# Loading and splitting attention's output weight inside attention instead of in the weights' part

## The reference

```
x = x + L0_xattn(layernorm(x), ctx, ctx)    # 16 heads of 32, softmax, with Wq, Wk, Wv, Wo, biases, temperature
x = x + L0_ffn(layernorm(x))                # 512 -> 2048 -> 512, weights and activations rounded to 8-bit steps
x = x + L1_xattn(layernorm(x), ctx, ctx)    # no softmax: scores * values, residual and layernorm inside
x = x + L1_ffn(layernorm(x))                # three 512 x 512 products, then tanh
```

## Time and profile before

| | us |
|---|---|
| median of three runs | 1871.63 |
| the profiled execution, its own time | 1874.35 |
| its span in the trace | 1872.6 |
| PE busy | 1791.1 (96%) |
| DVE busy | 1549.5 (83%) |
| ACT busy | 1239.9 (66%) |
| POOL busy | 954.1 (51%) |
| `prepare` / `attend` / `rest`, from first to last instruction | 0 to 172.0 / 172.3 to 945.9 / 947.4 to 1872.6 |

### The profile page before, as it was taken

One profiled execution on the slowest core, in us unless ns is written; L12 is line 12 of the kernel. 1 busy time (PEld: TensorE's weight loads), 2 busy tenths in 40 slices (PEclk: granted clock), 3 DMA queues, 4 the chain that ended last, 5 costly groups with the idle time before them and its releaser, 6 DMA issues. The chain is left out here.

```text
span 1872.6 us, 30344 instructions
## 1 busy us (share of the span) xinstructions
PE 1791.1 (96%) x9447; PEld 1345.5 (72%) x9530; DVE 1549.5 (83%) x3607; ACT 1239.9 (66%) x3379; POOL 954.1 (51%) x1053
## 2 busy tenths in 40 slices
PE   8997899999999999999879999899999999999997
PEld 7785688888888888888744444467677677767775
DVE  6765789999999999998769888888888888888875
ACT  4564899999999999999633333356555555565543
POOL 3121466666666666666610000156676666766664
PEclk9998999999999999999989999999999999999999
DMA  8377234544444444433379999064445445444311
GB/s 292 135 235 219 64 100 116 133 124 113 116 130 125 116 117 129 126 93 94 88 240 386 403 401 382 26 249 147 160 166 173 168 145 190 166 142 171 124 47 40
DMA packets 146927, 308.47 MB, mean 165 GB/s; under 512 B 44496, under 2 KB 56784, under 8 KB 129104
## 3 DMA queue, kind: packets, MB, share of 16 engines
q1 hardware_dynamic: 146624, 306.26, 50.3%
q10 hardware_dynamic: 144, 0.26, 0.1%
HBM read 165.95 MB, written 106.95 MB: 146 GB/s over the span
## 5 line engine op out<-in xcount | busy, mean ns | idle before, releaser
L1246 POOL TENSOR_TENSOR a_pr<-a_pr,a_rcp 128x512 f32<-128x512 f32 x256 | 266.8, 1042 | 283.2 <-DVE a_rcp L1092 283.0
L1002 ACT ACTIVATE a_pr<-a_s,a_nmax 128x128 f32<-128x128 f32 x1024 | 364.8, 381 | 15.7 <-DVE a_nmax L1085 14.0
L1495 PE MATMUL f_pair<-f_room,w 128*128 128x512 bf16 x999 | 224.6, 382 | 2.6 <-ACT f_room L1606 1.3
L1002 ACT ACTIVATION_READ_ACCUMULATOR a_pr<-a_s,a_nmax 128x1 f32 x1024 | 225.1, 220 | 0.0
L1937 POOL TENSOR_TENSOR f_ring<-f_ring,f_room 128x512 f32<-128x512 f32 x64 | 82.0, 1281 | 245.0 <-DVE f_room L1882 245.0
L1718 DVE CUSTOM_DVE_ANT_0 f_hf<-f_pair,nb,sh 128x512 f32<-128x512 f32 x244 | 172.0, 749 | 29.5 <-PE f_pair L1495 23.2
L1100 DVE TENSOR_TENSOR a_pTl<-a_pt,a_pTh 128x512 fp32r<-128x512 f32 x256 | 168.7, 680 | 19.8 <-ACT a_pTh L1014 19.1
L1085 DVE TENSOR_REDUCE a_nmax<-a_s 128x4 f32<-128x512 f32 x256 | 172.8, 675 | 13.9 <-PE a_s L892 13.6
L1495 PEld LDWEIGHTS f_pair<-f_room,w 128*128 128x128 bf16 x1024 | 99.4, 98 | 116.4 <-issue 3.0
L1650 ACT ACTIVATE f_room<-f_ring,f_off,f_rs 128x512 f32<-128x512 f32 x128 | 104.1, 813 | 114.2 <-POOL f_off L1928 113.3
L1922 POOL TENSOR_TENSOR f_rs<-f_rs,f_half 128x1 f32<-128x1 f32 x128 | 72.2, 564 | 187.2 <-DVE f_rs L1771 187.2
(11 more groups left out here) (392 smaller groups left out, 5141.6 us busy)
## 6 DMA issues: line engine op xcount, KB each, us to landing
hidden<-f_hf SPq DMA_DIRECT2D x57, 1024.0 KB, 9.4
f_hf<-hidden SPq DMA_DIRECT2D x57, 1024.0 KB, 5.2
xb<-x SPq DMA_DIRECT2D x16, 1024.0 KB, 5.7
a_qs<-bqreph SPq DMA_DIRECT2D x128, 128.0 KB, 2.4
a_qs<-bqrepl SPq DMA_DIRECT2D x128, 128.0 KB, 2.4
a_xr<-x SPq DMA_DIRECT2D x64, 256.0 KB, 3.7
x<-a_xr SPq DMA_DIRECT2D x64, 256.0 KB, 2.5
f_ring<-x SPq DMA_DIRECT2D x64, 256.0 KB, 4.8
```

What stands on the lines that cost most here:

```text
L1002: last = e.activation(pr[:, t, j, :], s_bank[t][:, j * P:j * P + P], ACT.Exp, bias=nmax[kk % 2][:, t, j:j + 1], accum_out=sums[kk % 2][:, ...
L1246: e.tensor_tensor(p, p, rcp[kk % 2][:, t, :].unsqueeze(2).to_broadcast([P, 4, KEYS]), ALU.mult).then_inc(*e_pn)
L1495: last = e.matmul(h_bank[(PAIRS * u + i) % 3][:, q, :], w1[:, k, f * P:f * P + P], xT[u % 2][:, k, :], start=k == 0, stop=k == KC - 1)
```

## The change

`WoT0` leaves the weights' part: the load, ACT's copy of 128x2048 and DVE's subtraction of 128x2048 go. Attention's SP issues it as four quarters of 256 KB into `xr[0..3]`, behind the first query tile's four transfers. ACT waits at the opening of step 0 for the four quarters and for `bo` together (one semaphore now counts all five transfers), and copies four tiles of 128x512 into `woh`. DVE makes the four low halves in step 3. Nothing else reads the `xr` tiles before: SP's first reload of x and PE's first output product wait for the low halves. In `rest` the four semaphores of the first tokens' quarters become one, which counts all four, so every quarter's relu waits for all of them.

In the weights' part, the lists of loads and slots:

```
-                 plain("A2"), w2_rows(3), x_rows[0], plain("WT"), plain("WqT0"), x_rows[1], plain("WoT0"), x_rows[2]]
-        BUF = [i % 3 for i in range(20)] + [0, 1, 2]
-        X_LOAD = {20: scr["e_x"][1], 22: scr["e_x"][0]}
+                 plain("A2"), w2_rows(3), x_rows[0], plain("WT"), plain("WqT0"), x_rows[1], x_rows[2]]
+        BUF = [i % 3 for i in range(20)] + [0, 2]
+        X_LOAD = {20: scr["e_x"][1], 21: scr["e_x"][0]}
```

and there ACT's call, DVE's call, and SP's loads ahead of and behind the eight stores:

```
-            weight(9, place["t"][-1])
...
-            weight(9)
...
-            load(21)
...
-            load(22)
+            load(21)
```

In attention, the semaphores, PE's `out`, ACT's `step`, DVE's `step` (behind `norm`), SP's `again` and SP's opening:

```
-        e_const, e_b = ev("const"), ev("bias", 16)
+        e_const, e_b, e_woh, e_wol = ev("const"), ev("outweight", 16 * (KC + 1)), ev("outhi"), ev("outlo")
...
+                if first(b) and o == 0:
+                    e_wol.wait_ge(e, KC - 1)
...
                 if opening:
+                    e_b.wait_ge(e, 0)
+                    for c in range(KC):
+                        e.activation(wo[0][:, c, :], xr[c][:], ACT.Copy).then_inc(*e_woh)
                     qhi(b, kk)
...
+                if first(b) and kk == 3:
+                    for c in range(KC):
+                        e_woh.wait_ge(e, c)
+                        e.tensor_tensor(wo[1][:, c, :], xr[c][:], f32(wo[0][:, c, :]), ALU.subtract).then_inc(*e_wol)
                 rc(b, kk, 1)
                 smax(b, kk, 2)
...
+                if first(b) and o == 0:
+                    e_wol.wait_ge(e, KC - 1)
...
             paired(0, -QUERY)
+            for c in range(KC):
+                e.dma_start(xr[c][:], A["WoT0"][cut(c), :]).then_inc(e_b.sem, 16)
             body_steps(e, step, LOAD, STORE + 1)
```

In `rest`, the semaphore, ACT's wait ahead of a relu, and SP's load of a quarter:

```
-        e_tok0, e_relu0 = [ev(f"first{t}", 16) for t in range(TPG)], ev("relu0")
+        e_tok0, e_relu0 = ev("first", 16 * TPG), ev("relu0")
...
-                        e_tok0[t].wait_ge(e, 0)
+                        e_tok0.wait_ge(e, 0)
...
-                e.dma_start(xb[0][:, t, :], x_g[0][:, t, :]).then_inc(*e_tok0[t])
+                e.dma_start(xb[0][:, t, :], x_g[0][:, t, :]).then_inc(e_tok0.sem, 16)
```

More of the change, by code:

```diff
@@ L116, in prepare @@
                  w1_rows(0), w1_rows(1), w1_rows(2), w1_rows(3), w2_rows(0), w2_rows(1), w2_rows(2), plain("A1T"),
-                 plain("A2"), w2_rows(3), x_rows[0], plain("WT"), plain("WqT0"), x_rows[1], plain("WoT0"), x_rows[2]]
-        BUF = [i % 3 for i in range(20)] + [0, 1, 2]
-        X_LOAD = {20: scr["e_x"][1], 22: scr["e_x"][0]}
-        W_LOAD, W_SLOT = (2, 3, 4, 5, 6, 14, 15, 18, 19, 21), (1, 2, 0, 1, 2, 0, 1, 2, 1, 0)
+                 plain("A2"), w2_rows(3), x_rows[0], plain("WT"), plain("WqT0"), x_rows[1], x_rows[2]]
+        BUF = [i % 3 for i in range(20)] + [0, 2]
+        X_LOAD = {20: scr["e_x"][1], 21: scr["e_x"][0]}
+        W_LOAD, W_SLOT = (2, 3, 4, 5, 6, 14, 15, 18, 19), (1, 2, 0, 1, 2, 0, 1, 2, 1)
         W_CENTRED = W_LOAD.index(5)
@@ L987, in _ @@
         def _(e):
-            e.dma_start(bo[:], A["L0_xattn_bo"].rearrange("(a n) -> a n", a=1).to_broadcast([P, D])).then_inc(*e_b)
+            e.dma_start(bo[:], A["L0_xattn_bo"].rearrange("(a n) -> a n", a=1).to_broadcast([P, D])).then_inc(e_b.sem, 16)
             def xhi(b, kk):
```

## The result

The changed kernel took 1880.27 us (median of 18 runs, 1875.31 to 1884.29), the kernel before 1874.32 us in the same series (18 runs, 1870.16 to 1879.64): 5.95 us more, a ratio of 1.0031 with a 95% interval of 1.0023 to 1.0039. The ratio lies just over the bound of 0.3% which the prediction had set for "slower". A second series gave 1881.71 against 1874.71, ratio 1.0036 (1.0024 to 1.0048). The sign was forecast; the size was three times the forecast +1.9.

The account below looks back on a forecast made before the run. Early attention steps are paced by a chain through ACT, DVE and PE, later ones by a full PE. Opening -1.0, step 3 +0.8 and `rest` +2.1 sum to +1.9: 1871.63 + 1.9 = 1873.5 us, range 1869.5 to 1877.8.

Parts of the forecast that it names:

- PE's clock: At attention's opening, PE stands still and restarts at the lower clock level as before; put at 0.
- Weights' part: End of the weights' part: without WoT0's copy and subtraction the border comes at 168.25, 4.0 us earlier.
- Opening: Attention's step 0: ACT waits for the weight's quarters, then copies; `qhi` begins 1.0 us earlier, bounds -3.7 to +1.9.
- Rival B: Attention's opening: fourth quarter lands at 182.95 behind a full queue; sum +7.4, 1879.0 us; chance 0.06.
- Rival A: Attention's opening: quarters land early, at 174.7, giving -3.7 there; sum -0.8, 1870.8 us; chance 0.14.
- Step 3: Attention's step 3: four added DVE subtractions, 2.48 us in a row, cost +0.8 us, bounds 0 to 1.75.
- the next 0.57 us have no more slack to go into: Attention's step 3: DVE work beyond the 1.91 us that `norm` takes in step 2 comes out in full.
- 0.24 + 0.57: Attention's step 3: 0.24 us that `norm` cost in step 2 plus the next 0.57 us, making +0.8.
- The weighing of POOL against DVE: Attention's step 3: POOL's overlap loses DVE 0.1 us; under an exclusive lock up to 1.04, the term +1.8.
- Opening of `rest`: Start of `rest`: four relus begin only when the fourth token quarter lands, +2.1 us, bounds 0.8 to 2.1.
- Rival C: Step 3 and `rest`'s opening: waits behind take up the added 0.8 or 2.1; sum -1.0, 1870.6 us; chance 0.10.
- A stage away from these three places: Rest of the kernel: no change forecast; one of over 2 us there would show the prediction wrong.

## Why the prediction was off, step by step

The sign was right and three of the terms held (border, plain delay of step 3, tokens). Two steps failed. The opening's term was mis-sized: -1.0 forecast, +0.2 measured in the table and +0.8 over more profiles. And PE's clock was put at nothing outside the opening, without a reason: behind step 3 a lowered clock added 0, 1.3 or 3.1 us in the three profiles, and at the end of attention, a place with no term at all, it stands beside +1.9 us.

**Weights' part: -4.0, right.** (-4.2 measured.) From the last fold to attention's first transfer the changed kernel takes 12.1 us, the kernel before 16.3.

**Opening: -1.0 forecast, +0.2 measured in the table; mis-sized.** (Counted with the kernels that share the opening, four profiles on either side, it is +0.8.) The mechanism (ACT waits for the weight, then copies) was right and the landing was wrong. Counted from attention's first transfer, the text had the fourth quarter issued at 3.8 us, landing at 9.1 and `qhi` at 11.1. Measured: 4.25, 10.64 and 12.73. Of the 1.6 us, 0.45 is the issue (the fourth quarter went 1.7 us behind the first, not the 1.3 of the earlier trace rows), 1.1 the landing (6.4 us against 5.25 of the earlier trace rows) and the rest the copies. The tokens' quarters were the nearest row by size, but they meet an idle queue; WoT0's stand behind x's third group, with the DMA share at 1.04 in 174 to 178. Rival B named that queue and overrated it. Rival A, an early landing, was not seen in any profile. The late copies recovered 4.7 us: with the border's -4.2 that leaves about +0.5 for the opening as the change has it, beside the +0.2 and +0.8 above.

**Step 3: +0.8 forecast; the plain part right, the clock left out.** `xlo` of step 3 came 12.30 us after that of step 2 (text: 12.2), and a step without lowered clock is 0.92 us longer. So the premise that "the next 0.57 us have no more slack to go into" held. The step that failed is the sum behind it, 0.24 + 0.57, which made the price a plain delay: I had asked about PE's clock at the opening alone, and with the lowered clock the two steps were 2.4 us longer in the mean of three profiles instead of 0.9. By the runs the block alone costs 2.2 us, and spreading it out saves 2.3. PE also shows a wait that was not there before: its transposes wait 0.66 us for POOL's product, which waits for the reciprocal behind the four. It comes shortly before the 1.66 us that PE stands for `xlo` anyway:

```profile
226.21 0.66 PE L902 MATMUL a_pt<-ident,a_pr 128*128 128x128 f32 x4 [0.66 <-POOL a_pr L1252]
228.96 0.50 PE L61 MATMUL a_qx<-a_xT1h,wqh 128*128 128x512 f32 x1 [1.66 <-DVE v1l L1081]
```

That this wait tips the clock is not shown: the wait is the same in the profile whose clock stayed at 1.00. The weighing of POOL against DVE there changed nothing: POOL's product ran from 221.55 to 222.59, the four began at 222.39 and took 2.55 us against the 2.48 of the earlier trace rows.

**Opening of `rest`: +2.1, right by the profiles** (+2.0 in the table); the runs give less, +1.0, +1.2 and +1.3 in three comparisons of medians. Rival C, that this and step 3's cost would not come out, is against the profiles: both do, and the stretch from the first product to the end is no shorter for it (915.4 us on average with four semaphores, 915.5 with one).

**"A stage away from these three places": wrong.** The end of attention takes 1.9 us more, by PE's clock. It was at 1.00 in the three profiles in which attention's steps are unchanged (42.4 to 43.0 us), and lower in all eleven with subtractions added in its first steps (43.7 to 46.3 us), 700 us earlier, the one with the block alone among them. The two repeats that were to tell chance from the change fell on the side of the change, but nothing was varied at that place, and three profiles are few on one side. Two things speak for caution. The row above it in the table is 1.0 us shorter, so that from `qhi` 5 to `rest` the changed kernel takes 0.9 us more, not 1.9. And both profiled executions of the kernel before had a mean granted clock of 0.988, as only 12 of its 88 runs in the series of experiments had; their mean is 0.9863. Over 1873 us these 0.0017 are 6.4 us more at the lower level, about as long as the one stretch here (6.8 us); where they lie is not on record. So a typical run of the kernel before may have the lowered stretch as well. Whether it belongs to the change, and how, stays open.

**The time.** Opening, step 3 and the end of attention miss by 1.2, 1.6 and 1.9 us: with +1.9 forecast that makes +6.6, and the table has +6.4. That the runs have nearly the same, +5.95 and +7.0, is partly luck, as the rows for step 3 and the end of attention depend on which executions were profiled, and one row of -1.0 without a cause stands between them. The range ended at 1877.8, 6.2 us over the median of three runs. Measured +5.95 lies inside this as a difference; the time of 1880.27 lies outside also because 18 runs put the kernel before at 1874.32, 2.7 us over its three-run median.

## What to carry to other kernels

A load that leaves a border still has to be waited for where its first user stands: put the consumer's wait behind the work that doesn't need it (here: copies after step 0, 4.7 us), not ahead of everything. Work given to the idle times of a paced loop was cheap in single pieces (one subtraction per step, about 0.2 us each) and dear in a block of four, behind which PE often ran at its lower clock; a pair was free in one step and not in another, so try the place and not only the size. And a difference that is to be predicted within 2 us needs a reference of more than three runs when these spread over 5.

## What the runs showed of the hardware that was not expected

The granted clock can fall or not fall in the same situation. Each us of the changed kernel around `xlo` of step 3 (columns as before):

```profile
225.00:226.00 1.00, 0.54 (x5) 0.34 (x3) 1.00 (x3) 0.62 (x3) 0.89 (x1) 1.00 0.97 203
226.00:227.00 1.00, 0.80 (x7) 0.80 (x8) 1.00 (x3) 1.00 (x8) 0.15 (x1) 1.00 0.18 39
227.00:228.00 1.00, 0.30 (x3) 0.06 (x1) 0.97 (x2) 0.81 (x4) 0.00 (x0) 1.00 0.55 121
228.00:229.00 1.00, 0.04 (x1) 0.04 (x1) 0.97 (x4) 1.00 (x3) 0.00 (x0) 1.00 0.65 141
229.00:230.00 1.00, 1.00 (x4) 0.82 (x5) 1.00 (x2) 1.00 (x6) 0.93 (x1) 0.78 0.00 0
230.00:231.00 1.00, 1.00 (x4) 0.81 (x3) 0.30 (x2) 0.83 (x6) 1.00 (x2) 0.50 0.00 0
```

and of its second profile, at the same point of the work:

```profile
224.51:225.51 1.00, 0.55 (x5) 0.34 (x3) 1.00 (x3) 0.61 (x3) 0.88 (x1) 1.00 0.97 203
225.51:226.51 1.00, 0.79 (x7) 0.79 (x8) 1.00 (x3) 1.00 (x8) 0.16 (x1) 1.00 0.17 39
226.51:227.51 1.00, 0.30 (x3) 0.07 (x1) 0.97 (x2) 0.81 (x4) 0.00 (x0) 1.00 0.55 121
227.51:228.51 1.00, 0.04 (x1) 0.04 (x1) 0.97 (x4) 1.00 (x3) 0.00 (x0) 1.00 0.66 141
228.51:229.51 1.00, 1.00 (x4) 0.82 (x5) 1.00 (x2) 1.00 (x6) 0.93 (x1) 1.00 0.00 0
229.51:230.51 1.00, 1.00 (x8) 0.90 (x7) 0.30 (x2) 0.83 (x6) 1.00 (x2) 1.00 0.00 0
```

Four us of equal activity, us by us, and then the clock goes to 0.50 (1.2 of 2.4 GHz) in one and stays at 1.00 in the other. In the last rows PE has 4 matmuls in its us at 0.50, and 8 at full clock. The Trainium skill (TensorE: Matmul & The Clock Gate, "What's actually happening") says that the activity is watched in windows that run freely and don't start with the kernel, so that the moment of a change varies. The two profiles agree with it as far as they go; that the phase of these windows decided here, no run shows. So such a cost is a chance and not a constant: behind the block of four in step 3, two lowered steps came in three profiles, one in two and none in one; without it (there nothing, single subtractions or a pair), none in seven. Ahead of step 3 they come without it too, in step 2 in three of the fourteen profiles.

It also shows in all the runs whose clock is on record, by the mean granted clock of each: 0.9863 for the kernel before (78 runs), 0.9849 for the changed kernel (18; 0.9845 in 8 more), 0.9851 with the block alone (12), 0.9868 with the subtractions spread (11), 0.9843 with the block twice (6).
